# A two-layer attention kernel: the written-out order of work on all five engines is replaced by another order

## The reference

```
h1 = layernorm(x);  x = attn(h1, h1; 16 heads of 16, q, k, v and the probabilities rounded to 8 bits) @ wo + bo + x
h2 = layernorm(x);  x = attn(h2, ctx; same form, 77 keys) @ wo2 + bo2 + x
h3 = layernorm(x);  a, g = split(h3 @ ff_w1 + b1);  x = (a * gelu(g)) @ ff_w2 + b2 + x
h  = rmsnorm(x);    x = x + gqa(h, rmsnorm(ctx); 16 heads of 64, 4 key heads, rotary, mask) @ Wo
h  = rmsnorm(x);    x = x + (silu(h @ Wgate) * (h @ Wup)) @ Wdown
```

## Time and profile before

| | |
|---|---|
| median of 3 runs | 2363.37 us (2362.61 to 2364.81) |
| the profiled execution | 2364.06 us, of which the span of instructions is 2362.3 us |
| busy: PE, DVE, ACT, POOL | 1911.3, 1839.2, 1128.3, 935.9 us |
| mean granted clock of TensorE | 0.893 |

### The profile page before, as it was taken

One profiled execution on the slowest core, in us unless ns is written; L12 is line 12 of the kernel. 1 busy time (PEld: TensorE's weight loads), 2 busy tenths in 40 slices (PEclk: granted clock), 3 DMA queues, 4 the chain that ended last, 5 costly groups with the idle time before them and its releaser, 6 DMA issues.

```text
span 2362.3 us, 35007 instructions
## 1 busy us (share of the span) xinstructions
PE 1911.3 (81%) x10552; PEld 1407.1 (60%) x10552; DVE 1839.2 (78%) x3327; ACT 1128.3 (48%) x1906; POOL 935.9 (40%) x1629
## 2 busy tenths in 40 slices
PE   4566578988989797989889898978798878978877
PEld 3223255766657575757667575756575665756665
DVE  1566869797988979797989889897979888795631
ACT  1244454545455555645454555555454644453211
POOL 1213335354443444443544434454434444342311
PEclk8676588998989898989999898989998998989998
DMA  7576444344535453434445353435334353433000
GB/s 232 122 139 135 86 86 98 77 87 82 100 69 104 76 113 77 94 76 87 89 74 101 74 117 77 93 72 108 69 67 89 70 114 63 83 68 64 1 11 5
DMA packets 658347, 203.77 MB, mean 86 GB/s; under 512 B 595387, under 2 KB 655535, under 8 KB 657903
## 3 DMA queue, kind: packets, MB, share of 16 engines
q1 hardware_dynamic: 654831, 201.52, 42.3%
q10 hardware_dynamic: 3328, 0.01, 0.1%
HBM read 43.76 MB, written 19.25 MB: 27 GB/s over the span
## 4 chain that ended last, share of the span: by engine, by line
PE 42%; DVE 36%; issue 11%; ACT 3%; DMA 3%; SPq 2%; POOL 2%; DVEq 0%; POOLq 0%; ACTq 0%
PE work L1353 20%; PE work L1363 15%; DVE scaled_row L1027 10%; DVE Pn L1045 7%; DVE scs L1115 2%; DVE lsum L1092 2%; DVE scs L1186 2%; DVE nmx L1109 2%; DVE p L1095 2%; DMA PT<-Pn 2%; PE rowps L1408 2%; DVE st L1050 2%; DVE lsum L1229 1%; PE outps L1435 1%; ACT E L881 1%
## 5 line engine op out<-in xcount | busy, mean ns | idle before, releaser
L881 ACT ACTIVATE E<-rowps,ebias,der 128x1024 f32<-128x1024 f32 x512 | 615.7, 1205 | 653.9 <-DVE scaled_row L1027 442.0
L1027 DVE TENSOR_SCALAR_CACHE_REDUCE scaled_row<-rowps,der 128x1024 uint8<-128x1024 f32 x512 | 645.8, 1276 | 94.7 <-PE rowps L1408 89.2
L1045 DVE TENSOR_SCALAR Pn<-E,rowinv 128x1024 int16<-128x1024 f32 x512 | 424.7, 843 | 144.4 <-DMA PT<-Pn 76.9
L722 POOL TENSOR_TENSOR rowden<-rowsum,raw 128x1 f32<-128x1 f32 x512 | 139.6, 273 | 644.5 <-ACT E L881 643.8
L725 POOL TENSOR_TENSOR rowinv<-rowden,minus 128x1 f32<-128x1 f32 x512 | 314.7, 615 | 92.3 <-POOL rowden L722 92.1
L1408 PE MATMUL rowps<-KC,QP 16*128 16x512 bf16 x1024 | 184.9, 419 | 120.3 <-ACT E L881 109.2
L1353 PE MATMUL work<-hTs,ff_w_sb 128*128 128x256 f32 x1024 | 235.8, 387 | 9.8 <-ACT hTs L855 9.8
L1353 PEld LDWEIGHTS work<-hTs,ff_w_sb 128*128 128x128 f32 x1024 | 193.0, 192 | 45.9 <-issue 19.5
L1408 PEld LDWEIGHTS rowps<-KC,QP 16*128 16x128 bf16 x1024 | 42.4, 92 | 243.7 <-ACT E L881 144.5
L1435 PE MATMUL outps<-PT,VB 128*16 128x256 f16 x2048 | 159.5, 308 | 5.9 <-DMA PT<-Pn 5.9
L1363 PE MATMUL work<-VW,pTs 128*128 128x256 f32 x640 | 159.8, 399 | 1.2 <-DVE pTs L1196 0.6
(11 more groups left out here) (143 smaller groups left out, 3164.8 us busy)
## 6 DMA issues: line engine op xcount, KB each, us to landing
PT<-Pn SPq DMA_TRANSPOSE x512, 3.1
VW<-vw_dram SPq DMA_DIRECT2D x8, 640.0 KB, 5.6
vw_dram<-scs SPq DMA_DIRECT2D x32, 154.0 KB
xa<-in_x SPq DMA_DIRECT2D x17, 256.0 KB, 3.0
QP<-q_dram SPq DMA_DIRECT2D x128, 32.0 KB, 2.1
oT<-OS SPq DMA_DIRECT2D x256, 16.0 KB, 1.8
xs<-in_x SPq DMA_DIRECT2D x16, 256.0 KB, 3.1
out<-xns SPq DMA_DIRECT2D x16, 256.0 KB, 2.3
```

Source lines behind the costliest of these rows:

```text
L722: nc.gpsimd.tensor_tensor(rowden[:, n:n + 1], rowsum[:, n:n + 1], raw[:, DW1:DW1 + 1], ALU.mult).then_inc(row_den.sem, 1)
L881: nc.scalar.activation(E[:, slot, :], rowps[n % 2][:], ACT.Exp, bias=ebias[:, n:n + 1], scale=der[:, AL1:AL1 + 1], accum_out=rowsum[:, n:n ...
L1027: nc.vector.tensor_scalar(scaled_row[:, n % 2, :], rowps[n % 2][:], der[:, NAL1:NAL1 + 1], 3.0e38, ALU.mult, ALU.min, accum_out=ebias[:, n ...
L1045: nc.vector.tensor_scalar(Pn[:, place, :], E[:, ring(k)[0], :], rowinv[:, k:k + 1], 255.0, ALU.mult, ALU.min).then_inc(row_round.sem, 1)
```

## The change

All five strings are replaced. TURNS becomes a table of kinds with one kind, "step", and `Runs` is a list that carries its kind; since KIND is empty, every step is of kind "step". The work itself, the waits and the buffers are as before.

```diff
-    "PE": (
-        "vrhhhrrphprprvpphrrhhhhllhrhhrhhhhrhvlrrvlhhhrllhhrhhhhrhllrhrhhhrvrlrlvhrllhhhhvrrlllllhlrllhrhhlrv"
-        "rlllllrrhrrllrl"),
-    "DVE": (
-        "nnpbpnbbnhnbbhnbbhnnhhhlbhhbhhhnhbnlhnhssnbnbhssllbnbhhnblnlbbnnbhbbnnlhllnlbllnblblnnhblnnlhbhhbbnn"
-        "nblbnnhbbnllbl"),
-    "ACT": ("eeepeeppeehpoeeeeehhhllhehheoleheheeeeoehllhleehhhllelleeelleellleoee"),
-    "POOL": ("iipiihpiiliiilhhhiliihhhlhhiiippiiiihiillilliiilhhhlhiiiiiii"),
-    "SP": ("tttthlhlhhtlttpthhthtttptttttttttppttttttttttth"),
+    "step": {
+        "PE": (
+            "vrhhhprrhprprpphvrrhhhhllrvhhhhrrhhhvhrlrlrhhhrllhhhhhhrrhllhhrhhrlvvlrrrhlrlhhhvhlllrllhlrrllhh"
+            "hlrrvlllllrrhrrllrl"),
+        "DVE": (
+            "npbnpnbbhnnbbhnbnhnbhhhlnbhhhlnbhhbhnhhbssnbnshsnlbblnhhblnbnlbhnbhbblnnllnblllnnlbblnhbnlhbhlhn"
+            "bbnnnbblhnbhnnbblll"),
+        "ACT": "eeepeeppeehpoeeeeohhelhhelehheehheeleoeeehllhhlehhlleleleelleolelleee",
+        "POOL": "ipiiiihipiplilihhiihihhhllihhiipiihiiililliliiihlhiihhiiiiil",
+        "SP": "htlthlthhttthhlthttppttttttttpptttttttttttttttth",
+    },
 }
+KIND = {}
...
-    for letter in TURNS["PE"]:
+    for letter in TURNS[kind]["PE"]:
...
-ORDER = item_order()
+ORDER = {kind: item_order(kind) for kind in TURNS}
...
-    for k, (c, i) in enumerate(ORDER):
+    for k, (c, i) in enumerate(ORDER[chains.kind]):
...
-            take_turns(order, use)
+            take_turns(TURNS[runs.kind][engine], use)
```

More of the change, by code:

```diff
@@ L62 @@
 TURNS = {
-    "PE": (
-        "vrhhhrrphprprvpphrrhhhhllhrhhrhhhhrhvlrrvlhhhrllhhrhhhhrhllrhrhhhrvrlrlvhrllhhhhvrrlllllhlrllhrhhlrv"
-        "rlllllrrhrrllrl"),
-    "DVE": (
-        "nnpbpnbbnhnbbhnbbhnnhhhlbhhbhhhnhbnlhnhssnbnbhssllbnbhhnblnlbbnnbhbbnnlhllnlbllnblblnnhblnnlhbhhbbnn"
-        "nblbnnhbbnllbl"),
-    "ACT": ("eeepeeppeehpoeeeeehhhllhehheoleheheeeeoehllhleehhhllelleeelleellleoee"),
-    "POOL": ("iipiihpiiliiilhhhiliihhhlhhiiippiiiihiillilliiilhhhlhiiiiiii"),
-    "SP": ("tttthlhlhhtlttpthhthtttptttttttttppttttttttttth"),
+    "step": {
[4 more added lines that the diff above has]
+            "npbnpnbbhnnbbhnbnhnbhhhlnbhhhlnbhhbhnhhbssnbnshsnlbblnhhblnbnlbhnbhbblnnllnblllnnlbblnhbnlhbhlhn"
+            "bbnnnbblnhbnnbblll"),
+        "ACT": "eeepeeppeehpoeeeeohhelhhelehheehheeleoeeehllhhlehhlleleleelleolelleee",
+        "POOL": "ipiiiihipiplilihhiihihhhllihhiipiihiiililliliiihlhiihhiiiiil",
+        "SP": "htlthlthhhttthhlttppttttttttpptttttttttttttttth",
+    },
 }
+KIND = {}
 PRE_AT = {"tr": (4.0, 4.9), "q": (5.5, 6.9), "k": (6.3, 7.8), "v": (7.2, 8.7)}
@@ L80, in item, with __init__, item_order @@
     return [i for i, x in enumerate(items) if x[0] == name][n]
-def item_order():
+class Runs(list):
+    def __init__(self, chains, v=None):
+        super().__init__(chains)
+        self.kind = KIND.get(v, "step")
+def item_order(kind):
     begins = {c: {sum(x[2] for x in ITEMS[c][:i]): i for i in range(len(ITEMS[c]))} for c in ITEMS}
     turn, out = {c: 0 for c in ITEMS}, []
-    for letter in TURNS["PE"]:
+    for letter in TURNS[kind]["PE"]:
         c = PARTS_OF.get(letter)
@@ L421, in shifted @@
                     yield half + by
-            by_time(*[shifted(pre(eng, u, ["pre"]), FIRST_EVERY * u) for u in range(LEAD)], *early)
+            by_time(*[shifted(pre(eng, u, Runs(["pre"])), FIRST_EVERY * u) for u in range(LEAD)], *early)
         def all_steps(eng, step, pre, early=(), before_attention=lambda: None, before_last=lambda: None):
@@ L444, in all_steps, with run_step @@
             loop(U + 1, U + 2, high=True)
-        def run_step(parts, eng, v, order, attention, setup, pre, low, high, sums=None):
-            runs = [c for c in ITEMS if parts[c]]
+        def run_step(parts, eng, v, engine, attention, setup, pre, low, high, sums=None):
+            runs = Runs([c for c in ITEMS if parts[c]], v)
             if parts["setup"]:
@@ L681, in step @@
             def step(v, parts):
-                run_step(parts, sp, v, TURNS["SP"], {"t": attn_sync(sp, v, parts)}, setup_sync, pre_sync, low_sync, high_sync)
+                run_step(parts, sp, v, "SP", {"t": attn_sync(sp, v, parts)}, setup_sync, pre_sync, low_sync, high_sync)
                 if parts["setup"]:
@@ L830, in step @@
             def step(v, parts):
-                run_step(parts, pool, v, TURNS["POOL"], {"i": inverses(pool, v, parts)}, setup_pool_part, pre_pool, low_pool, high_pool)
+                run_step(parts, pool, v, "POOL", {"i": inverses(pool, v, parts)}, setup_pool_part, pre_pool, low_pool, high_pool)
                 if parts["setup"]:
@@ L993, in step @@
             def step(v, parts):
-                run_step(parts, act, v, TURNS["ACT"], {"e": exponentials(act, v, parts), "o": outputs(act, v, parts)},
+                run_step(parts, act, v, "ACT", {"e": exponentials(act, v, parts), "o": outputs(act, v, parts)},
                          setup_act_part, pre_act, low_act, high_act)
@@ L1333, in step @@
             def step(v, parts):
-                run_step(parts, dve, v, TURNS["DVE"], {"b": biases(dve, v, parts), "n": roundings(dve, v, parts)},
+                run_step(parts, dve, v, "DVE", {"b": biases(dve, v, parts), "n": roundings(dve, v, parts)},
                          setup_dve_part, pre_dve, low_dve, high_dve, high_sums)
@@ L1644, in step @@
             def step(v, parts):
-                run_step(parts, pe, v, TURNS["PE"], {"r": rows_of_scores(pe, v, parts), "v": values(pe, v, parts)},
+                run_step(parts, pe, v, "PE", {"r": rows_of_scores(pe, v, parts), "v": values(pe, v, parts)},
                          setup_pe, pre_pe, low_pe, high_pe)
```

## The result

The changed kernel takes 2356.24 us (median of 9 runs, 2353.85 to 2360.71); the kernel before took 2364.81 in the same session (9 runs, 2362.61 to 2368.21). The ratio is 0.9965 with the interval 0.9955 to 0.9976: faster by 0.35%, where 2378.8 and "slower" were forecast. The profiled execution took 2354.36 us for a span of 2352.6; it is at the lower end of runs that scatter over 7 us.

A forecast was written before the change was run, and what follows sets the result against it. It took each step as a DVE stage followed by a PE stage; 0, +0.1, -2.47 + 0.66 and +2.8 made +1.1 us a step, 15 us over 14 steps, giving 2378.8 us, range 2350 to 2400.

The forecast's parts named there:

- the end of the step: DVE from down's addition to a3: two more roundings and a 1.5 us landing wait, 10.25 us instead of 7.45, +2.8 a step.
- The prediction's own signs: Profile marks: down's addition waits 3 to 5 us, last rounding about 1.5, ffo 2.5 to 3; ffo under 1 means wrong sign.
- What bounds the kernel: Each step is a DVE stage (61 us), then a PE stage (68.2 us), with hand-overs at pp3 and wo.
- The middle, -2.47: Middle of PE stage: rows 26 and 28 moved, waits ahead of tr1, row 28 and g0 gone, -2.47 us a step.
- Hand-over, +0.66: At pp3, tiles 20 and 21 are rounded back to back, POOL's cast ends one rounding later: +0.66 us a step.
- The rival: At the hand-over POOL gets in between the two roundings, so +0.66 becomes 0: 2369 us, chance 0.12.
- Start of the step, +0.1: Step start: bias0 may meet tile 5's rounding, 0 to +0.9, taken as +0.1 us; moved SP loads and stores 0.
- DVE stage, 0: From the addition after wo to sm3: same turns, no gain or loss taken; bounds +0.9 and -2.7 us a step.
- about as many meetings: DVE stage: roundings stretched by POOL operations, up to 0.9 us each, counted about as many in the new order.
- A granted clock that falls further is no case of its own: Clock 0.86 in DVE stage, 0.97 in PE stage; moved V products lie in the former, where PE has 12 us spare.
- One step for fourteen: The sum of +1.1 us a step was applied alike to steps 2 to 15: 14 x 1.1 = 15 us.

The follow-up runs named there:

- E1: Changed kernel with DVE's turn of down ahead of tile 28's rounding, so three roundings instead of two follow down's addition: 2406.72 us, 1.0172 of the kernel before.
- E6: Changed kernel with DVE's last 18 turns put back as in the kernel before: 2347.21 us, 0.9921 of the kernel before.
- E23: Not a run: a turn of ACT, an exponential, standing ahead of the copy pt2.4 in the changed kernel, where it waits 0.81 us for DVE's max23.
- E9: Changed kernel with SP's string and DVE's last 18 turns as before, plus ACT's pt2.4 ahead of E23 and DVE's pt2.3 ahead of max24: 2331.32 us.
- E10: Changed kernel with SP's string and DVE's last 18 turns as before, plus tile 21's rounding back behind pt2.3: 2340.39 us, 0.9891 of the kernel before.
- E5: Changed kernel with SP's string of the kernel before, other four strings new: 2347.91 us, 0.9925 of the kernel before.
- E3: Old strings up to the last p, pt2.4 and pp3, new ones from there on, SP's old string: 2354.74 us, 0.9945 of the kernel before.
- E11: Kernel before with only the part between the last p and a0 changed: 2340.88 us, 0.9893 of the kernel before.

## Why the prediction was wrong

**The step that failed is the end of the step: +2.8 us for the turn of down ahead of two roundings and for a wait for a landing.** It was worked out for a miscopied string. That order, run as E1, has the chain of 10.3 us and the 1.44 us wait as forecast, in seven of ten steps. The real order has one rounding more behind down, +0.66, and no wait for a landing; E6 takes the 0.66 back. With the same working and the real string the sum is 0 + 0.1 + 0.66 - 2.47 + 0.66 = -1.05 us a step, -15 us, 2349: the sign is settled by this reading alone. The result lies between that and no change. The prediction's own signs say the same: ffo waits 0.83 us, under the 1 us that it named, the last rounding waits for no transfer, and the cast takes 1.05 us and not 1.7. The wait of down's addition, 3.16 us, came in the forecast's 3 to 5, but two orders share it.

The other steps, with what was measured:

- *What bounds the kernel.* Right: the DVE stage, then the PE stage. That DVE's order between down and a3 is on the chain was right too: E6 and E1 move ffo by what the chain changes.
- *The middle, -2.47.* 2.70, right in place and size. Not foreseen: o2 waits for pt2.4 behind E23, which E9 took away.
- *Hand-over, +0.66.* Measured 0. POOL's cast starts 0.25 to 0.44 us behind the first rounding and gets its turn before the second; that one is stretched. One pair of rows (where rowinv began beside two roundings and ended with them) had been let speak for another operation. The rival was right, and E10 confirms it: with one rounding there instead of two the hand-over takes the same 3.29 us. By the Trainium skill, "SBUF — State Buffer", section "SBUF: two separate sides", the shared pair goes to whoever starts first, for the whole instruction. The trace agrees here: the first rounding keeps its 0.75 us, the cast takes 1.05 instead of 0.70, and the second rounding 1.19 instead of 0.75. Why rowinv in the earlier trace rows, which began only 0.05 us behind the first rounding, did not get in between is not shown by any run.
- *Start of the step, +0.1, with SP's moves at 0.* Measured +1.1: 0.36 in ordinary steps and 2.7 in those that begin a batch. In five of the seven ordinary steps the rounding of tile 5 meets bias0 and takes 1.5 to 1.7 us, and the addition after wo comes 26.1 to 26.3 us behind ffo; in the two without the meeting it is 0.75 us, and 25.75. So this meeting, priced at 0.1, costs 0.4 where it happens. The 2.7 is SP's, and E5 takes 2.3 of it back. The prediction looked at step 7, in which `u % PARTS` skips K1 and VW, and priced the moved loads by it. The one step in four that issues them has another queue.
- *DVE stage, 0.* Measured +0.40, within the bounds, but "about as many meetings" was wrong. In step 4 of the kernel before three of the stage's 13 roundings take 1.6 to 1.7 us; in the changed kernel one does (1.73), and DVE is busy for 57.2 us instead of 57.8. The stage is as long all the same (58.74 and 58.75), since DVE now waits 0.5 us for POOL's `rs` (L753) and 0.2 us ahead of another rounding: fewer meetings came, and their gain did not. The +0.40 has two sources. 1.3 of the 4.1 us in ten steps is in step 2, where one rounding more meets a POOL product (L800) and takes 1.71 us; most of the rest is in steps 6 and 7 (60.2 and 60.1), whose low stretch of the clock lies 23 us behind the addition after wo, as in E3. "A granted clock that falls further is no case of its own" was wrong. It doesn't fall further here, it falls elsewhere.
- *One step for fourteen.* The sum took one value for steps 2 to 15. Steps 2 to 11 gain 0.34 us each and steps 12 to 15 gain 1.3; why is open.
- *No rival named the clock's place.* By the readings above it takes most of the 12 us that E11 misses of its 38, and most of E3's missing 18.

Of E1, the order that the forecast was for, it would have said 2378.8; it takes 2406.7, above the range. PE's idle time ahead of ffo costs more than itself, since the clock then is low (0.61 in the 3.4 us behind it).

## What to carry to other kernels

Before working out what an order does, take it from the file by a program and let each generator's turns be named and counted; an oddity in a copy (a letter with nothing to do) is first of all a copying error. Price a moved transfer in the rarest step that issues it, not in the one at hand. And when a chain of two stages gets shorter, expect the low stretches of TensorE's clock to move against the work: read which matmuls they fall on before and after, and what waits for those.

## What was not expected of the hardware

- Of two runs with the same order and starts equal to 0.01 us, one had its low stretch of clock (6.8 us at 0.50) 8 us later than the other. Steps with it there took 1.4 to 2.4 us more in a stage of 58.7. What had differed was ahead of it: 0.7 us more of PE idle before ffo and a shorter stage before that. What exactly moves it was not found.
- 2.0 us of PE idle ahead of ffo (E1) were followed by 3.4 us at a granted clock of 0.61, and 18.8 us up to Wq where it is 16.7 otherwise.
- POOL's cast came in between two roundings that DVE ran back to back: 1.05 us for the cast, which takes 0.70 alone, and 1.85 us for the pair that takes 1.41.
- Of the DVE stage's roundings one instead of three took 1.6 us or more beside work of POOL. DVE was busy for 0.6 us less, and the stage did not get shorter.
